# Unit q and k and the levels of layer 0: split into fp16 rows and turned by transposing DMAs

## The reference

```python
# layer 0 attention, on layernorm(x):
Qp = query @ Wq + bq
K = l2norm(key @ Wk + bk);  Q = l2norm(Qp);  V = value @ Wv + bv
out = softmax(Q K^T * SCALE) @ V @ Wo + bo
x = x + layernorm(out + Qp) * gamma + beta
# layer 0 feed-forward, on layernorm(x):
xh = x @ Hadamard
q = clip(round(xh / scale), -8, 7) * scale     # the levels, 4 bits
x = x + q @ ternary(weight).T
# layer 1: attention without l2norm (scores clipped at 1e4),
# then gelu(x @ ternary(W1).T + b1) @ ternary(W2).T + b2
```

## Time and profile before

| | |
|---|---|
| median of 3 runs | 1841.64 us (1840.3 to 1843.56) |
| span of the profiled execution | 1838.4 us |
| instructions | 45922 |
| granted TensorE clock, mean | 0.978 |

### The profile page before, as it was taken

The page is one execution under the profiler, slowest core; times in us unless marked ns, Lnnn a source line. Parts: engine busy times, 40 slices in busy tenths (PEclk is TensorE's granted clock), DMA queues, the critical chain, the costliest instruction groups (busy, mean ns, idle before and its releaser), DMA issues. The chain is left out here.

```text
span 1838.4 us, 45922 instructions
## 1 busy us (share of the span) xinstructions
PE 1722.9 (94%) x18714; PEld 1052.9 (57%) x18714; DVE 1209.7 (66%) x2446; ACT 1067.7 (58%) x1970; POOL 925.6 (50%) x1062
## 2 busy tenths in 40 slices
PE   5789999999999999999999999979769999999999
PEld 2455666666666666666666666655544444444443
DVE  5658778687786867768687786849973433344332
ACT  5675866868677586876868667576552222222221
POOL 1663846748466484755848467464462222222221
PEclk9789999999999999999999999989979999999999
DMA  7122020211202112020220202045320111011100
GB/s 234 44 86 80 6 96 2 96 51 47 96 2 97 42 56 96 3 96 21 77 92 6 96 2 97 17 158 189 106 97 0 47 47 46 1 46 47 46 24 23
DMA packets 46343, 115.56 MB, mean 63 GB/s; under 512 B 5420, under 2 KB 9644, under 8 KB 45112
## 3 DMA queue, kind: packets, MB, share of 16 engines
q1 hardware_dynamic: 43832, 104.25, 16.4%
q0 software_dynamic: 2304, 8.39, 1.1%
HBM read 72.78 MB, written 31.46 MB: 57 GB/s over the span
## 5 line engine op out<-in xcount | busy, mean ns | idle before, releaser
L759 POOL TENSOR_TENSOR arena<-arena 128x512 f16<-128x512 f32 x512 | 568.8, 1135 | 159.2 <-ACT arena L913 159.1
L905 ACT ACTIVATE arena<-psum 128x512 f32<-128x512 f32 x512 | 309.8, 612 | 54.4 <-PE psum L1430 31.3
L913 ACT ACTIVATE arena<-arena 128x512 f16<-128x512 f32 x512 | 329.2, 651 | 1.0 <-PE psum L1465 1.0
L963 ACT ACTIVATE arena<-psum,arena 128x512 f32<-128x512 f32 x128 | 88.3, 690 | 352.6 <-PE psum L1483 352.6
L1289 PE MATMUL psum<-arena 128*128 128x512 f16 x672 | 258.2, 384 | 7.5 <-ACT arena L905 4.0
L1290 PE MATMUL psum<-arena 128*128 128x512 f16 x672 | 255.4, 380 | 0.0
L1293 PE MATMUL psum<-arena 128*128 128x512 f16 x672 | 255.0, 379 | 0.0
L789 POOL TENSOR_TENSOR arena<-arena 128x512 f16<-128x512 f32 x64 | 73.1, 1142 | 341.4 <-DVE arena L1233 341.4
L1483 PE MATMUL psum<-arena 128*128 128x512 f16 x1024 | 243.6, 380 | 1.4 <-DVE arena L1226 1.4
L1493 PE MATMUL psum<-arena 128*128 128x512 f16 x1016 | 239.9, 378 | 1.0 <-POOL arena L789 1.0
L1233 DVE CAST arena<-arena 128x512 f16<-128x512 f32 x128 | 54.8, 428 | 271.8 <-ACT arena L963 271.8
(11 more groups left out here) (123 smaller groups left out, 3329.5 us busy)
## 6 DMA issues: line engine op xcount, KB each, us to landing
arena<-in_x SPq DMA_DIRECT2D x32, 512.0 KB, 4.6
arena<-x_scratch SPq DMA_DIRECT2D x32, 512.0 KB, 5.7
arena<-in_L_ffn_W SPq DMA_DIRECT2D x16, 1024.0 KB, 5.2
arena<-arena SPq DMA_DIRECT2D x16, 512.0 KB, 6.5
x_scratch<-arena POOLq DMA_DIRECT2D x16, 512.0 KB, 6.2
x_scratch<-arena SPq DMA_DIRECT2D x16, 512.0 KB, 3.0
out<-arena SPq DMA_DIRECT2D x14, 512.0 KB, 3.8
arena<-in_ctx SPq DMA_DIRECT2D x16, 384.0 KB, 5.7
```

What stands on the lines that cost most here:

```text
L759: gp.tensor_tensor(pl[l][:, h % NP, :], pf[l][:, h % NF, :], ph[l][:, h % NP, :], ALU.subtract).then_inc(p_lo[l].sem, 1)
L905: sc.activation(pf[l][:, h % NF, :], bank(u.bank), ACT.Exp, scale=SCALE / (QS * QS) if l == 0 else SCALE).then_inc(read[u.bank], 1)
L913: sc.activation(ph[l][:, h % NP, :], pf[l][:, h % NF, :], ACT.Copy).then_inc(p_hi[l].sem, 1)
```

## The change

What it does: q is projected for both tiles, then k for both tiles. `unit` writes the upper fp16 half of the scaled rows on ScalarE, and VectorE computes the remainder from the fp32 rows in SBUF (a new instruction in place of the subtraction from PSUM). Both halves lie side by side in the tile `xn0`. A new task `unit_turn` on SP issues one transposing DMA for each tile of q, later of k: [128, 1024] fp16 into the turned halves. `turn_levels` becomes a transposing DMA of [128, 512] fp16 on SP. The tasks of TensorE, ScalarE and VectorE for turning and splitting q and k of layer 0 and the levels are gone. Waits on the old signal of the split halves become waits on the landing of the DMAs: the next load of x waits for it, the first scores of a batch, and ScalarE's `unit` of k for q's DMAs, since it writes the same rows. All digits of the orders are new: the steady list has 189 tasks instead of 195, and load 1 stands ahead of load 0. One constant takes 8 words instead of 1.

```diff
-    for k in ks:
+    for j in range(2):
         late = []
-        for j in (1, 0):
+        for k in ks:
             out += [("project", 0, k, j, 0)] + late + [("project", 0, k, j, 1)]
             late = [("bias", 0, k, j)]
-        out += late + [("norm", 0, k), ("unit", 0, k)]
-    for k in ks:
-        out += [("turn_qk", 0, k, j) for j in range(2)] + [("split_qk", 0, k, j) for j in range(2)]
+        out += late + [("norm", 0, j), ("unit", 0, j), ("unit_turn", 0, j)]
...
+        qk_rows = [[a.bitcast(F16).rearrange("p (j c n) -> p j c n", j=2, c=2 * DC) for a in qk_raw[0]]][0]
+        unit_rows = xn0.bitcast(F16).rearrange("p t (s n) -> p t s n", s=2)
...
# SP
-                    sp.wait_ge(qk_hi[0].sem, qk_hi[0].at(b - 1))
+                    sp.wait_ge(qk_turned.sem, qk_turned.at(b - 1))
...
+                    elif kind == "unit_turn":
+                        j = at[0]
+                        if j == 0 and b > 1:
+                            sp.wait_ge(p_hi[0].sem, p_hi[0].at(b - 2))
+                        for k in range(NT):
+                            sp.wait_ge(unit_lo.sem, unit_lo.at(b, 2 * j + k + 1))
+                            sp.dma_start_transpose(qk_rows[(odd - ALL.index(part)) % 2][:, j, :, k * P:(k + 1) * P],
+                                                   unit_rows[:, k].rearrange("p s n -> p (s n)")).then_inc(qk_turned.sem, 16)
+                    elif kind == "turn_levels":
+                        sp.wait_ge(nq_ready.sem, nq_ready.at(b, at[0] + 1))
+                        sp.dma_start_transpose(cols4(nT, at[0]), nq[:, at[0], :]).then_inc(levels_turned[at[0]].sem, 16)
...
# ScalarE
                     elif kind == "unit":
-                        k = at[0]
-                        act.wait_ge(norms.sem, norms.at(b, k + 1))
-                        for j in range(2):
-                            src, dst = ((qf0[:, k, :], xn[0][:, k, :]), (kf0[:, k, :], kf0[:, k, :]))[j]
-                            sc.activation(dst, src, ACT.Copy, scale=rn[:, 2 * k + j:2 * k + j + 1]).then_inc(unit.sem, 1)
+                        j = at[0]
+                        act.wait_ge(norms.sem, norms.at(b, j + 1))
+                        if j == 1:
+                            act.wait_ge(qk_turned.sem, qk_turned.at(b, 16 * NT))
+                        for k in range(NT):
+                            sc.activation(unit_rows[:, k, 0, :], (qf0, kf0)[j][:, k, :], ACT.Copy,
+                                          scale=rn[:, 2 * j + k:2 * j + k + 1]).then_inc(unit.sem, 1)
...
# VectorE
+                    elif kind == "unit":
+                        for n in range(NT):
+                            dve.wait_ge(unit.sem, unit.at(b, 2 * k + n + 1))
+                            v.scalar_tensor_tensor(out=unit_rows[:, n, 1, :], in0=(qf0, kf0)[k][:, n, :],
+                                                   scalar=rn[:, 2 * k + n:2 * k + n + 1], in1=unit_rows[:, n, 0, :],
+                                                   op0=ALU.mult, op1=ALU.subtract).then_inc(unit_lo.sem, 1)
...
# TensorE
-                    elif kind == "turn_qk":
-                        j = at[1]
-                        pe.wait_ge(unit.sem, unit.at(b, 2 * k + j + 1))
-                        turn(use["qt", 0, k, j], (xn[0], kf0)[j][:, k, :], DC)
...
                     elif kind == "scores":
+                        if l == k == 0:
+                            pe.wait_ge(qk_turned.sem, qk_turned.at(b))
...
-                    elif kind == "turn_levels":
-                        pe.wait_ge(nq_ready.sem, nq_ready.at(b, k + 1))
...
                     elif kind == "ffn0":
...
-                        open_bank(u, use["nt", 0, k])
+                        pe.wait_ge(levels_turned[k].sem, levels_turned[k].at(b))
+                        open_bank(u)
```

More of the change, by code:

```diff
@@ L103, in fills @@
     kind, l, *at = task
-    names = {"turn_x": "x", "turn_ctx": "c", "turn_qk": "qt", "project_turned": "qt", "turn_out": "ot",
-             "out_project": "y", "turn_ffn": "xf", "hadamard": "had", "turn_levels": "nt", "ffn0": "f0",
+    names = {"turn_x": "x", "turn_ctx": "c", "project_turned": "qt", "turn_out": "ot",
+             "out_project": "y", "turn_ffn": "xf", "hadamard": "had", "ffn0": "f0",
              "tern_sum": "tw", "tern_turn": "tt", "mean_sum": "ms", "turn_signs": "sg"}
@@ L1073, in step @@
                         j = at[1]
-                        if l == 0 and first and (k, j) == (0, 1):
+                        if l == 0 and first and (k, j) == (0, 0):
                             dve.wait_ge(rows_loaded, 32)
@@ new lines, in step @@
+                    elif kind == "unit":
[4 more added lines that the diff above has]
+                                                   op0=ALU.mult, op1=ALU.subtract).then_inc(unit_lo.sem, 1)
+                    elif kind == "split_qk":
+                        j, m = at
+                        u = use["qt", 1, j, m]
+                        upper, lower = halves(1, odd, part)
+                        dve.wait_ge(qk_hi.sem, qk_hi.at(b, 2 * (1 - j) + m + 1))
+                        v.scalar_tensor_tensor(out=lower[:, j, 2 * m:2 * m + 2, :],
+                                               in0=bank(u.bank).rearrange("p (m n) -> p m n", m=2), scalar=1.0 / WS,
+                                               in1=upper[:, j, 2 * m:2 * m + 2, :], op0=ALU.mult,
+                                               op1=ALU.subtract).then_inc(read[u.bank], 1)
@@ L1383, in step @@
                         mm.then_inc(filled[u.bank], 1)
-                    elif kind == "turn_levels":
-                        pe.wait_ge(nq_ready.sem, nq_ready.at(b, k + 1))
-                        u = use["nt", 0, k]
-                        open_bank(u)
-                        for c in range(DC):
-                            mm = te.transpose(bank(u.bank).bitcast(F16)[:, c * P:(c + 1) * P], nq[:, k, c * P:(c + 1) * P], identh)
-                        mm.then_inc(filled[u.bank], 1)
                     elif kind == "ffn0":
@@ L1400, in step @@
                     elif kind == "values_ready":
-                        turned = [use["qt", 0, k, j] for k in range(NT) for j in range(2)] if l == 0 else []
-                        all_read(pe, turned + [use["qkv", l, k, 2] for k in range(NT)])
+                        all_read(pe, [use["qkv", l, k, 2] for k in range(NT)])
                         pe.nop()
```

93 lines of the change are left out of this document (35 added, 58 removed).

## The result

The changed kernel takes 1851.35 us (median, 1850.22 to 1853.95) against 1841.2 us for the kernel before on the same chip: ratio 1.0055, 95% interval 1.0041 to 1.0069, so slower by 10 us. The forecast was 1806.1, and 1851 lies outside its range. The profiled execution of the changed kernel spans 1848.4 us, 10.0 more than before; the profiles are compared by their spans.

A forecast was written before the change was run, and what follows sets the result against it. The prediction took TensorE, busy 76.1 of 78.2 us, to bound the steady iterations: -30.5 - 2.3 - 1 - 5 + 2 + 1.3 = -35.5 us from 1838.4 gives 1802.9, plus 3.2 to the median: 1806.1, range 1792 to 1848.

The forecast's parts named there:

- The step that failed: Steady iterations 3 to 15: TensorE work removed shortens the 78.28 us period one for one; 2.35 us an iteration.
- -30.5 and -2.3: Gain from transposes taken off TensorE: 30.5 us over 13 steady iterations, 2.3 us in iteration 2.
- The standing time I let stay at 2.1 us: Steady period: TensorE stands idle 2.1 us, expected to remain so after the change.
- the order leaves gaps: Steady periods: TensorE's standing time grows; doubled gives 1833 us, 3.5 us more gives 1852; 13%, of which 5% no faster.
- The sign that I gave for it: Steady period staying at 78 us, with TensorE's idle time up to 4.5 us, would show the forecast wrong.
- VectorE's remainder: Four scaled subtractions from SBUF replace four from PSUM at 0.682 us: +0.4 us each, 1.6 us an iteration on VectorE.
- Its effect on the path: VectorE's new subtractions stretch GpSimd's heads: 0.1 us an iteration, 1.3 us in all (0 to 8).
- The DMAs: Transposing [128 x 1024] takes 3.3 to 5 us, half that for [128 x 512]; hidden in the steady part.
- the slow rival: Transposing DMAs at a third of copy rate, 10 us each, make ffn0 wait; +180 us, about 1985 us; 9%.
- ScalarE's waits for the turned levels: ScalarE's 9.0 us of waiting an iteration for levels turned by TensorE goes away; counted as no gain.
- Iteration 16: The new order hides TensorE's 6.95 us stall for the context's load behind five more tasks: -5 us (0 to -9).
- The fill: Iteration 1: levels, DMA and ffn0 follow each other closely, so the DMAs cost +2 us (0 to 4).

The follow-up runs named there:

- e14: e4 with 18 fp32 transposes fewer on TensorE an iteration from batch 4 on, output not the reference's; 1840.08 us, ratio 1.0003 to the kernel before.
- e4: The changed kernel with the orders of iterations 17 and 18 alone taken from the kernel before; 1842.38 us, ratio 1.0017 to the kernel before.
- e12: The kernel before with 18 fp32 transposes fewer on TensorE an iteration from batch 4 on, output not the reference's; 1831.57 us, ratio 0.9956.
- e10: e4 with VectorE's remainder of the unit rows replaced by a short multiplication by zero, output without lower halves of q and k; 1837.51 us.
- e1: The kernel before with one constant taking 8 words instead of 1, so later SBUF tiles move by 28 bytes; 1840.97 us against 1839.86.
- e9: e4 with the exponentials of both layers and GpSimd's fp16 halves moved to odd word addresses; 1837.41 us against 1841.47 for the kernel before.
- e8: The kernel before with only the new order of iteration 16; 1836.04 us, ratio 0.9982.
- e15: e4 with 18 fp32 transposes more on TensorE an iteration from batch 4 on; 1862.27 us, ratio 1.0119 to the kernel before.
- e16: e4 with the odd addresses of e9 and the short VectorE instruction of e10 together; 1837.12 us, ratio 0.9988 to the kernel before.
- e2: The changed kernel with 16 words instead of 8 for the constant, so later tiles start at multiples of 64 bytes; 1850.83 us, ratio 1.0059.
- e6: e4 with both layers' exponentials and layer 1's fp16 halves at odd words, layer 0's halves left aligned; 1838.22 us against 1839.0 for the kernel before.
- e11: e4 with the levels turned by TensorE and copied by ScalarE again instead of by DMA; 1884.89 us, ratio 1.024 to the kernel before.
- e17: e16 with 18 fp32 transposes fewer on TensorE an iteration from batch 4 on; 1831.37 us, ratio 0.9962 to the kernel before.
- e13: The kernel before with 18 fp32 transposes more on TensorE an iteration from batch 4 on; 1858.13 us, ratio 1.01.

## Why the prediction was wrong, point by point

**The step that failed** is the one in the first paragraph, "a microsecond of work taken off TensorE there is a microsecond of the period, as long as nothing else comes late", and the sum that rests on it, -30.5 and -2.3. I read 76.1 of 78.2 us busy as a bound. It was one for work that is added, not for work that is taken off. Measured in the old order, with no wait, bank or DMA changed, 1.94 us were worth 0.66. In the new order they were worth 0.9 in periods with the same clock, and 0.04 on average, because the clock fell in 10 of e14's iterations 5 to 15 and in 1 of e4's. The prediction has no term for a fall of the clock. The standing time I let stay at 2.1 us; by spacing of starts it was 4.5 to 4.7 already, since the busy time is made of modelled lengths, which reach into the gaps. It became 7.1.

**The rival that came** is the second, the order leaves gaps: I gave 1852 for 3.5 us more of standing in a period, and 5% to the part of it at or above the old time. The mechanism was right, with 2.4 us more standing in the period and the rest from the drain; the chance was far too low. The sign that I gave for it came as well: a period of 78.6 us, of which TensorE is not busy for 3.9 (78.60 less 74.69). The waits of the kernel before did not give its price: of the 27 waits of the attend matmuls for GpSimd only 3, 1.0 us in all, lie in the ten steady periods, the others in the fill and the drain. What would have told is e12 and an order tried for itself.

**The costs elsewhere.** The two iterations of the drain have their own digits and I counted nothing for them; they are +8.6 us by the span, and with the old digits in e4 the stretch is 9.2 us shorter, the largest single item of the loss. I had looked at what the new digits of iterations 0 and 16 did and not at 17 and 18. VectorE's remainder I had at +0.4 us on 0.682: the estimate said 1.08, the row shows 0.915, and the longest in the period from 411.8, beside GpSimd's subtractions, 1.48. Its effect on the path I had at 1.3 us, and e10 has it at about 5, inside my 0 to 8. "One constant takes 8 words" stands in the change as I described it, and I passed over it; e1 and e9 show that it is worth 7% of GpSimd's main instruction, nothing clear in the old order and at most some 4 us in the new one (e9 against e4 by spans), of which 1.7 lie in the steady part.

**What held.** The DMAs: landing in 3.2 and 2.5 us, hidden everywhere in the steady part; the slow rival was false. ScalarE's waits for the turned levels, are gone, and brought nothing, as booked. Iteration 16: -5.8 for -5, and e8 shows that 3 us of it come from its order. The fill: +0.4 us to the end of iteration 2 where I had -0.3 (-2.3 for iteration 2, +2 for the fill).

**What the sum should have been.** By the periods at a clock of 1.00: the new order with its DMAs at equal load, e15 beside the kernel before, +1.9 us, in 13 iterations +25; the load taken off again, e15 to e4, -1.4 x 13 = -18; together +6.5, where +6.7 was measured. With the fill at +0.4, iteration 16 at -5.8 and the rest at +8.6 that is +10, as measured; but these three are the measured differences themselves, and only the drain's has a run that gives it a cause (e4), as e8 has for 3 of the 5.8. The shift and the remainder are part of the first term, 0.4 and 0.3 us a period at a clock of 1.00 (e9 and e10 against e4), 1.0 together (e16).

## What to carry to other kernels

Busy at 97% of a period is a bound on making it longer, not on making it shorter: before booking a gain for work taken off, take the work out by itself in a version whose output doesn't matter, as e12 did, which costs one run. Look at the granted clock of each period before you average them: here means of ten periods hid that one kernel's clock fell in 10 iterations of 11 and the other's in 1, and the work taken off looked worthless. A change that moves buffers and rewrites orders has parts that its purpose doesn't name: every order string has its iterations and every allocation ahead of others shifts them, and both need a term in the sum. And try the parts singly: here one of them, the order of iteration 16, beats both kernels by itself (1836.04), as does the changed kernel with the old drain and odd addresses (1837.41).

## What the runs showed of the hardware

- GpSimd's subtraction of [128 x 512] fp32 and fp16 into fp16 has a median of 1.09 us with its operands one word (4 bytes) past a multiple of 32 bytes, the only odd place tried, and 1.16 us at multiples of 32 or 64 bytes (e1, e2; both lengths in one program in e6 and e9): the better aligned addresses are the slower ones.
- A transposing DMA of [128 x 1024] fp16 within SBUF lands after a median of 3.2 us, one of [128 x 512] after 2.5, but the issue holds SP's queue for 1.2 to 1.7 us in the steady period (up to 2.9 elsewhere), about three times the 0.48 of a plain one. The Trainium skill, "DMA: Bandwidth & Descriptors", section "DMA Transpose (X-bar)", wants SBUF addresses at multiples of 32 bytes for it, which no run here tried to do without. The constant of 8 words puts the tiles there, and GpSimd's 1.16 us come with it.
- VectorE's scaled subtraction on SBUF has a median of 0.74 us and took up to 2.08 us in the changed kernel, 0.915 on average, where the plain subtraction from PSUM had 0.682.
- A granted clock below 1.00 for part of the first 24 us after the store of x1 made a period longer by 0.9 to 1.9 us against periods of the same kernel without it (e4, e9, e10, e11, e14, e15, e16, e17). It came in none of the iterations 5 to 15 of the kernel before, e12 and e13, in 1 of e4's 11, 6 of e16's, 9 of e17's and 10 of e11's and e14's. e11 has a stop of 1.8 us ahead of each store; e14 has none and only 1.94 us less of transposes than e4. e14 differs from e4 in the number of transposes alone, so there the falls come with the work taken off; by what way is open, and e12, with the same work taken off in the old order, has none. In e16 nearly the same busy time of TensorE in the 8 us after the store (6.06 and 6.05 us) was followed by 1.00 in one iteration and by 0.79 in the next.
